# A decoder layer on one core: the engines' loop over twelve of sixteen batches written out as straight code, its waits on constants

## What is computed

```python
def mixer(x):                       # L0_attn
    h = silu(causal_conv4(x @ in_w.T + in_b))          # 512 channels
    xp = h @ xp_w.T + xp_b
    a = exp(-exp(xp[..., :16])); b = silu(xp[..., 16:]) * h.sum(-1, keepdims=True)
    ys = scan(state = state * a_t + b_t)               # over the 256 tokens
    return ys @ out_w.T + out_b
def cross(ctx, lat):                # L0_xattn, 8 heads of 128
    xn, ln = layernorm(ctx), layernorm(lat)
    q = ln @ Wq + bq; k, v = split(concat([xn, ln]) @ Wkv + bkv)   # 77 + 256 keys
    return softmax(q k^T / sqrt(128)) v @ Wo + bo
def experts(x):                     # 8 experts, top 2, at most 512 tokens each
    weights = softmax over the two highest of x @ expert_embeddings.T
    return scatter_add(weight * (relu(x[index] @ W1[e]) @ W2[e]))
x = layernorm(x + mixer(x))
x = layernorm(x + cross(ctx_1024, x))
x = layernorm(x + experts(x))
```

## Time and profile before

| | |
|---|---|
| median of 3 runs | 1131.69 us (1128.64 to 1133.58) |
| time of the profiled execution | 1132.4 us |
| its span, first to last instruction | 1130.6 us |
| mean granted TensorE clock | 0.951 |
| busy PE, PEld (weight loads) | 1012.9, 941.6 us |
| busy DVE, ACT, POOL | 805.9, 665.4, 507.1 us |
| instructions in the trace | 23058 |

### The profile page before, as it was taken

The page is one execution under the profiler, slowest core; times in us unless marked ns, Lnnn a source line. Parts: engine busy times, 40 slices in busy tenths (PEclk is TensorE's granted clock), DMA queues, the critical chain, the costliest instruction groups (busy, mean ns, idle before and its releaser), DMA issues.

```text
span 1130.6 us, 23058 instructions
## 1 busy us (share of the span) xinstructions
PE 1012.9 (90%) x6878; PEld 941.6 (83%) x6878; DVE 805.9 (71%) x2021; ACT 665.4 (59%) x1713; POOL 507.1 (45%) x826
## 2 busy tenths in 40 slices
PE   2479999999999999999999999999999999379970
PEld 1368999999999999899989998999999888269960
DVE  2557787778777877777778777877877776345435
ACT  2447666666666666566656665666575665145535
POOL 1422435363536353635364536453654443425553
PEclk7689999999999999999999999999999999679995
DMA  9240203010301030103010301030103000475548
GB/s 305 89 166 21 78 23 103 24 62 16 106 24 56 15 109 24 54 15 112 21 54 15 112 21 54 15 112 21 54 17 104 21 31 10 154 239 84 79 50 300
DMA packets 60335, 83.95 MB, mean 74 GB/s; under 512 B 13940, under 2 KB 43688, under 8 KB 60264
## 3 DMA queue, kind: packets, MB, share of 16 engines
q1 hardware_dynamic: 52584, 70.46, 18.9%
q0 software_dynamic: 7680, 12.72, 5.4%
HBM read 44.16 MB, written 38.99 MB: 74 GB/s over the span
## 4 chain that ended last, share of the span: by engine, by line
PE 69%; ACT 10%; DVE 8%; issue 6%; DMA 3%; POOL 2%; SPq 1%; ACTq 0%; DVEq 0%; POOLq 0%
PE ps L546 19%; PE ps L548 18%; PE ps L547 18%; PE ps L573 6%; PE ps L631 3%; PE ps L639 3%; ACT prob L919 2%; DVE nmx L1302 2%; PE ps L679 1%; ACT fx L999 1%; ACT pT_hi L934 1%; ACT k_hi L808 1%; ACT x2T L862 1%; DMA oww<-in_out_w 1%; ACT ut L835 1%
## 5 line engine op out<-in xcount | busy, mean ns | idle before, releaser
L1478 POOL TENSOR_SCALAR prob<-prob,rinv 128x333 f32<-128x333 f32 x256 | 142.4, 568 | 364.4 <-DVE rinv L1311 363.7
L546 PE MATMUL ps<-kv_lo,w_hi 128*128 128x256 f32 (+1 forms) x512 | 159.1, 311 | 4.8 <-DVE vst_lo L1007 1.9
L914 ACT ACTIVATE oT_hi<-ps 128x256 fp32r<-128x256 f32 x128 | 49.2, 385 | 193.3 <-PE ps L548 193.3
L548 PE MATMUL ps<-kv_hi,w_hi 128*128 128x256 f32 (+1 forms) x512 | 153.9, 301 | 0.0
L547 PE MATMUL ps<-kv_hi,w_lo 128*128 128x256 f32 (+1 forms) x512 | 153.5, 300 | 0.0
L919 ACT ACTIVATE prob<-ps,nmx 128x333 f32<-128x333 f32 x256 | 135.0, 537 | 17.8 <-DVE nmx L1302 17.7
L1007 DVE TENSOR_TENSOR pT_lo<-ps,pT_hi 128x512 fp32r<-128x512 f32 (+1 forms) x256 | 130.3, 551 | 0.6 <-ACT pT_hi L934 0.6
L1302 DVE TENSOR_REDUCE nmx<-ps 128x2 f32<-128x666 f32 x128 | 108.4, 847 | 29.7 <-PE ps L548 16.8
L573 PE MATMUL ps<-ident,prob 128*128 128x128 f32 (+1 forms) x768 | 109.0, 273 | 10.5 <-DVE oT_lo L1007 10.4
L546 PE MATMUL ps<-pT_lo,v_hi 128*128 128x256 f32 (+1 forms) x384 | 108.5, 283 | 0.9 <-DVE pT_lo L1007 0.9
L548 PE MATMUL ps<-pT_hi,v_hi 128*128 128x256 f32 (+1 forms) x384 | 108.3, 282 | 0.0
(11 more groups left out here) (223 smaller groups left out, 3007.4 us busy)
## 6 DMA issues: line engine op xcount, KB each, us to landing
wraw<-in_W SPq DMA_DIRECT2D x14, 512.0 KB, 6.7
vcd_hi<-vst_hi SPq DMA_DIRECT2D x10, 512.0 KB, 2.7
vcd_lo<-vst_lo SPq DMA_DIRECT2D x10, 512.0 KB, 3.5
v_hi<-vcd_hi SPq DMA_DIRECT2D x32, 154.0 KB
v_lo<-vcd_lo SPq DMA_DIRECT2D x32, 154.0 KB
slots<-initr SPq DMA_DIRECT2D x8, 520.0 KB, 8.4
xts<-in_xT SPq DMA_DIRECT2D x16, 256.0 KB
xs<-in_x SPq DMA_DIRECT2D x16, 256.0 KB
```

What stands on the lines that cost most here:

```text
L546: pe.matmul(dst, hi1, lo2, start=first, stop=False, skip_group_check=True)
L548: return pe.matmul(dst, hi1, hi2, start=False, stop=last, skip_group_check=True)
L914: act.activation(oT_hi[:, h % 2, :], ps[:, AVB, 0:S], ACT.Copy).then_inc(oTh_set, 1)
L1478: pool.tensor_scalar(prob[:, h % 2, t, 0:KEYS], prob[:, h % 2, t, 0:KEYS], rinv[:, h % 2, t:t + 1], 1.0, ALU.mult, ALU.mult).then_inc(norm ...
```

## The change

The loop of six rounds becomes a Python loop, so that each engine's program holds the twelve bodies one behind the other, with `i` a Python int. Every wait on a value that stood in a register is now a wait on a constant, and `need_apart` no longer increments `passed`. What each engine computes, and in what order, stays.

```diff
@@ -360,7 +360,7 @@
             body(-2, 0, {"aft"}, set(), 0)
             body(-1, 1, {"aft", "nxt", "ctx", "more"}, {"aft"}, 0)
             body(0, 0, {"att", "aft", "nxt", "ctx"}, had, 2)
-            with eng.Fori(0, (B - 4) // 2) as i:
+            for i in range((B - 4) // 2):
                 body(2 * i + 1, 1, mid | {"ctx"}, had, i + 3)
                 body(2 * i + 2, 0, mid, had, i + 3)
             body(B - 3, 1, mid | {"ctx"}, had, CT - 1)
```

## The result

The changed kernel took 1118.40 us (median of 4 runs, 1115.75 to 1120.46), the kernel before in the same job 1130.97 (4 runs, 1128.64 to 1133.58). The ratio is 0.9887, with a 95% interval of 0.9855 to 0.9918: faster by 1.1%, some 12.6 us. I had forecast 1122.6 us and a gain of 9.1, with a range of 1118.7 to 1126.7.

A forecast was written before the change was run, and what follows sets the result against it. PE was taken to bound the kernel, held up by DVE's branches. Gains of 7.5 + 1.0 + 0.6 = 9.1 us off the profiled 1132.4 gave 1123.3, less 0.7 for the median: 1122.6 us, range 1118.7 to 1126.7.

The forecast's parts named there:

- The branch's stall on DVE: At DVE's five taken branches back, before nmx in slot 0 of odd bodies: removing them gives 7.52 us.
- Another engine next in line: ACT's, POOL's or SP's register and branch instructions, possibly showing in slot 0 once DVE's stall goes: costed at nothing.
- Waits on registers, odd bodies: Body 1 against body 13, same work: 0.17 us each, 1.02 us for the six odd loop bodies.
- Waits on registers, even bodies: Six even loop bodies, no straight one to compare: 0.1 us each, 0.6 in all, bounded by nothing and 1.02 us.
- Body 14's clock: PE's clock falls behind its wait for k_lo; if the fall doesn't come, 1.5 us more gain, 1121.1 us.
- Fetches cost nothing: Straight code adds some 42 instruction packets on q8, read as PE's, costed at nothing.
- straight code stalls at blocks: Rival: PE stalls on entering new instruction blocks, up to 1.5 us each, 42 of them, 63 us, 1186; slower had chance 0.04.
- the stall isn't the branch's: Rival: DVE still waits before nmx for something else, only the registers' 1.6 us comes, 1130.1 us; chance 0.04.

The follow-up runs named there:

- e16: Kernel before, loops kept, with 26 semaphore increments put on DVE ahead of its loop: 1120.45 us against 1130.02, ratio 0.9927.
- e1: Kernel before with only DVE's twelve bodies written out straight, the other engines still looping: 1120.79 us against 1132.14, ratio 0.9907.
- e2: Changed kernel's straight code on four engines, but DVE keeps its loop with register waits: 1128.30 us, ratio 0.9973 to the kernel before.
- e9: As e2, but DVE's loop has three rounds of four bodies: 1128.90 us against 1137.51 for the kernel before, ratio 0.9928.
- e14: Kernel before with 70 semaphore increments put on DVE ahead of its loop: 1130.29 us, ratio 0.9991.
- e15: Kernel before with 128 semaphore increments put on DVE ahead of its loop, as a control: 1132.79 us, ratio 1.0013.
- e5: Kernel before with only PE's twelve bodies written out straight, the other engines still looping: 1128.66 us against 1130.91, ratio 0.9979.
- e10: Kernel before, unchanged, run again for a second trace; it and e11 took 1136.38 and 1134.46 us.
- e11: Kernel before, unchanged, run again for a third trace; e10 and it took 1136.38 and 1134.46 us.
- e3: Kernel before with its loop of six rounds split into six loops of one round on every engine: 1118.10 us, ratio 0.9881.
- e6: Changed kernel with a two-round loop of one semaphore increment on DVE ahead of nmx in five odd bodies: 1117.15 us, ratio 0.9878.
- e7: Changed kernel with six DVE loops of 60 to 360 semaphore increments behind its last transfer; whole time not given, 3.2 us extra a round at 360.
- e8: Changed kernel with the expert stage's loops on PE and POOL written out too: 1117.50 us, ratio 0.9885 to the kernel before.
- e12: As e7, with 304 to 348 increments; whole time not given, extra time a round at 312, 328 and 348 only.

## Why the prediction was right in kind and short in size

The forecast gain was 9.1 us; it is 12.6 between the medians and 13.4 between the two profiled executions. The mechanism held. What failed is the size of two terms: the waits on registers in the even bodies, put at 0.6 us with an upper bound of 1.0, gave 2.0, and the clock of body 14, put at nothing in the sum, gave 1.60 between the two traces. Of the 4.3 us that are missing from the forecast by the traces these two make 1.4 and 1.6; the odd bodies make 0.4, and the rest is 0.06 in body 13 and 0.81 ahead of body 1 and behind body 14.

- **The branch's stall on DVE**, 7.52 us forecast. Right. e16 takes away the stalls and nothing else, and bodies 1 to 12 go from 673.69 to 666.39: 7.30 us. PE's wait for oT_lo, which I gave as 1.26 us each, is 1.20 to 1.42 us.
- **Another engine next in line**, costed at nothing: right by e1, where four engines still branch and no rest stays in slot 0.
- **Waits on registers, odd bodies**, 1.0 us forecast. Short. From e16, which has them, to the changed kernel: 57.01 - 56.75 = 0.26 us a body, 1.6 us. My 0.17 came from body 13, which isn't quite free of them (56.82 us, and 56.76 in the changed kernel), and was one difference of two bodies taken six times.
- **Waits on registers, even bodies**, 0.6 us forecast with 1.0 as the upper bound. This is the step that failed by the most inside the loop: from e16 it is 54.0 - 53.7 = 0.3 us a body, 2.0 us against the first trace. I bounded it by the odd bodies since the even ones have no context tile and so fewer waits. But PE doesn't pay by the number of waits; it pays where one makes it late, and the even bodies have such a place of their own, slot 3 (6.41 us before, 6.29 after). There DVE goes from q_lo to nmx, th and oT_lo without a pause, and PE's transposes wait for oT_lo. In body 4 of the kernel before:

```profile
322.47 0.41 PE L573 MATMUL ps<-ident,prob 128*77 128x128 f32 x2 [0.22 <-DVE oT_lo L1007]
```

  In the changed kernel this wait is 0.10 us, and the odd bodies have no such wait in slot 3. It is 0.12 of the 0.3 us; the rest is in slots 0, 4 and 7, where the odd bodies pay too. The two terms together are 3.6 us by 666.39 - 662.76, and I had 1.6. This holds the waits on registers with all that goes with them, the register instructions, the increments of `passed` and the branches that hide; no run takes these apart.
- **Body 14's clock.** I gave the case that the fall doesn't come as 1.5 us more, at the edge of the likeliest case, and left it out of the sum. It measured 1.60. Of the traces with DVE's stalls, five have the fall (the first, e2, e9, e14, e15) and three don't (e5, e10, e11); of the ten without stalls none has it (the three of the changed kernel, e1, e3, e6, e7, e8, e12, e16). PE's wait ahead of it is the same, 1.62 us in the changed kernel against 1.68. The view of windows behind that wait, against the last of the earlier trace rows:

```profile
882.30:885.70 3.40, 3.40 (x28) 3.40 (x27) 2.46 (x9) 1.07 (x3) 1.04 (x1) 1.00 0.01 2
```

  So the fall is seen only with stalls, in five of eight traces, and why isn't known; 5/8 of 1.60 us, about 1 us of the difference of the medians, is an estimate of what it is worth. That it came in the first pair is in part luck.
- **Fetches cost nothing** in straight code: right. q8 has 55 packets instead of 23, 32 more and not 42 (the old loop's first round has 6 packets itself, and a straight pair 6 or 7), and it is PE's: with PE in the loop (e1) it has 23 again. No body is longer for them.
- **The rivals.** That straight code stalls at blocks: no. That the stall isn't the branch's: the branch alone indeed isn't enough (e6), but with a loop over four blocks it is what the stall comes with. The Trainium skill (Runtime: NRT & Kernel Launch, section Instruction fetch mechanics) was right that a taken branch out of what is held makes an engine wait, and that straight code hides its fetches. Its size of 512 instructions for DVE is not what these runs show: the loop of 351 (I had counted 322 rows) was not held where it stood.
- **The range** ended 0.3 us too high, at 1118.7 against 1118.40. That end had room for 1.0 us from the even bodies, for body 14's 1.5 and for 2 us between medians; the bound on the even bodies is the one that didn't hold, by 1.0 us.

## What to carry to other kernels

A loop on an engine is cheap as long as nothing has to be fetched on its way back; find out by the instruction queues of the profile (no packets in a round, or some at each way back), and look for issue time at the loop's line on engines that you think have slack, since a stall of 2.4 us on DVE, busy for 71%, cost PE 1.5 us each time. When a trace has a stretch of the same work in the new form, as body 13 was here, its length is a better forecast than a sum over instructions, and where it is lacking (the even bodies) the bound has to be wide. A stall can be removed by moving a loop's start, without writing it out: that gave 7.3 of the 10.9 us in bodies 1 to 12.

## What the runs showed of the hardware

- DVE's instructions come in packets of 8 KB, which by their distance in time are 128 instructions. Loops of up to 336 increments that lie in three blocks cost 0.3 to 0.5 us a round beside their increments and fetched nothing; those that touch four had five packets a round and paid 3.2 to 4.6 us more on each way back. In the kernel DVE stood still for 2.3 to 2.6 us between v_lo and nmx. PE's packets are 16 KB, and it fetched nothing in a loop of 779 matmuls with their weight loads.
- 26 semaphore increments in idle time, ahead of everything, made the kernel before 0.7% faster, and 70 or 128 did nothing.
- A semaphore increment on DVE takes 0.094 us.
- Waits on registers, with the instructions that go with them, cost 3.6 us in twelve bodies, 0.3 us each, spread over several engines.
